# Second attention and last expert stage: two blocks in a row, or one block in which they take turns

## The reference, cut to what matters

```
x = x + xattn1(layernorm(x), ctx)          # 16 heads of 64, 64 context keys plus one null key, then a layernorm
n = x * rsqrt(mean(x^2) + 1e-8) * norm_w   # of layernorm(x)
x = x + relu(n @ sw1 + sb1) @ sw2 + sb2    # shared expert, all rows
      + sum over the 2 best of 8 experts of gate * (relu(n @ ew1[e] + eb1[e]) @ ew2[e] + eb2[e])
```

## Time and profile before

| | us |
|---|---|
| time, median of 3 runs | 1447.45 (1446.88 to 1448.34) |
| span of the profiled execution | 1468.5 |
| PE busy | 1250.4 (85%) |
| DVE busy | 1054.3 (72%) |
| ACT busy | 899.3 (61%) |
| POOL busy | 653.5 (44%) |

### The profile page before, as it was taken

The page is one execution under the profiler, slowest core; times in us unless marked ns, Lnnn a source line. Parts: engine busy times, 40 slices in busy tenths (PEclk is TensorE's granted clock), DMA queues, the critical chain, the costliest instruction groups (busy, mean ns, idle before and its releaser), DMA issues. The chain is left out here.

```text
span 1468.5 us, 35946 instructions
## 1 busy us (share of the span) xinstructions
PE 1250.4 (85%) x13401; PEld 1041.2 (71%) x13401; DVE 1054.3 (72%) x2080; ACT 899.3 (61%) x1699; POOL 653.5 (44%) x677
## 2 busy tenths in 40 slices
PE   4999998399999999997599999999997268999880
PEld 3777777278777877786489888888886256787660
DVE  5888888566877687675256678989887369676563
ACT  3888887566565666654355655666654248787660
POOL 2222222145655555564332345556755327165561
PEclk9999999689999999999699999999999669999995
DMA  4222221332213221321210000000000123146646
GB/s 143 93 94 93 94 93 64 116 94 80 73 39 92 80 73 37 94 80 44 86 38 17 10 17 9 17 15 18 24 13 17 44 58 89 48 151 217 203 139 182
DMA packets 88373, 109.64 MB, mean 75 GB/s; under 512 B 13322, under 2 KB 55050, under 8 KB 88202
## 3 DMA queue, kind: packets, MB, share of 16 engines
q1 hardware_dynamic: 83210, 97.05, 21.3%
q0 software_dynamic: 4992, 10.30, 2.1%
HBM read 61.70 MB, written 29.82 MB: 62 GB/s over the span
## 5 line engine op out<-in xcount | busy, mean ns | idle before, releaser
L830 POOL TENSOR_TENSOR b_h_lo<-b_h,b_h_hi 128x512 fp32r<-128x512 f32 x168 | 216.3, 1292 | 179.7 <-ACT b_h_hi L854 179.2
L849 ACT ACTIVATE b_zg<-b_zg 128x512 f32<-128x512 f32 x168 | 97.6, 581 | 82.0 <-PE b_zg L894 81.8
L854 ACT ACTIVATE b_h_hi<-b_h 128x512 fp32r<-128x512 f32 x168 | 105.2, 626 | 65.7 <-DVE b_h L1059 65.6
L1059 DVE TENSOR_TENSOR b_h<-b_zg,b_uw 128x512 f32<-128x512 f32 x168 | 116.2, 692 | 32.1 <-ACT b_zg L849 26.8
L2173 POOL DMA_INDIRECT planes_dram<-d_y_out,d_back x92 | 94.5, 1028 | 93.6 <-DVE d_y_out L2484 68.8
L1052 DVE TENSOR_TENSOR b_uw<-b_zu,b_gw 128x512 f32<-128x512 f32 x128 | 88.2, 689 | 57.7 <-PE b_zu L894 50.9
L2453 DVE TENSOR_TENSOR d_h_lo<-d_h,d_h_hi 128x512 fp32r<-128x512 f32 x124 | 85.1, 689 | 44.6 <-ACT d_h_hi L2214 26.8
L312 POOL TENSOR_TENSOR a_qx<-a_qT,headmask 128x256 f32<-128x256 f32 x64 | 37.9, 612 | 150.3 <-ACT a_qT L347 150.3
L519 DVE TENSOR_REDUCE a_top<-a_score_ps 128x8 f32<-128x1024 f32 x64 | 78.1, 1220 | 18.6 <-PE a_score_ps L410 18.6
L1293 POOL TENSOR_TENSOR c_prob<-c_prob,c_recip 128x512 f32<-128x512 f32 x64 | 65.5, 1044 | 50.9 <-DVE c_recip L1709 50.9
L1716 DVE TENSOR_TENSOR c_oT_lo<-c_oy,c_oT_hi 128x512 fp32r<-128x512 f32 x64 | 43.7, 683 | 58.1 <-ACT c_oT_hi L1421 57.5
(11 more groups left out here) (393 smaller groups left out, 4172.3 us busy)
## 6 DMA issues: line engine op xcount, KB each, us to landing
rows_dram<-a_blank SPq DMA_DIRECT2D x32, 520.0 KB, 3.3
b_gw<-gates_dram SPq DMA_DIRECT2D x64, 256.0 KB, 3.9
d_up_slot<-d_up_tab SPq DMA_DIRECT2D x15, 512.0 KB
d_down_slot<-d_down_tab SPq DMA_DIRECT2D x15, 512.0 KB
d_xg<-rows_dram SPq DMA_DIRECT2D x23, 260.0 KB
b_gm<-gates_dram SPq DMA_DIRECT2D x32, 160.0 KB, 3.8
c_craw<-in_c_ctxT_dram SPq DMA_DIRECT2D x16, 256.0 KB, 3.1
d_pay<-planes_dram SPq DMA_DIRECT2D x12, 256.0 KB, 4.3
```

Of the source, the lines that this page charges most:

```text
L830: pool.tensor_tensor(h_lo[:, m % HS, :], h[:, m % HF, :], h_hi[:, m % HS, :].bitcast(F32), ALU.subtract).then_inc(lo_done.sem, 1)
L849: act.activation(zg_ps[:, n % ZG, :], zg_ps[:, n % ZG, :], ACT.Silu).then_inc(sg_done.sem, 1)
L854: act.activation(h_hi[:, m % HS, :], h[:, m % HF, :], ACT.Copy).then_inc(hi_done.sem, 1)
L1059: dve.tensor_tensor(h[:, n % HF, :], zg_ps[:, n % ZG, :], uw[:, n % 2, :], ALU.mult).then_inc(h_done.sem, 1)
```

## The change

Both stages become generators, one for each engine, and share one block, one PSUM tensor (`arena`) and a memory plan (`Room`: the tiles of the last stage lie where tiles of the attention have been used up). `in_turn` runs them in a written order. The attention runs 38 ticks alone, -6 to 31 (ACT 37). Then steps of the last stage and ticks take turns:

```diff
+        order = [(1, 4), (0, 1), (1, 4)] + [(0, 1), (1, 3)] * 5 + [(0, 1), (1, 1)] * 3
+        for quarters in (1, 2, 1, 2, 1, 2, 1, 2, 2):
+            order += [(0, 1), (1, quarters)]
+        order.append((1, 4 * (TILES + 3)))
+        alone = 38
...
+            in_turn([(0, alone - 1)] + order, first.scalar(act), second.scalar(act))
...
+            in_turn([(0, alone)] + order, first.vector(dve), second.vector(dve))
```

All eight groups are routed by the attention; the router of the last stage, its three `pay` buffers and its `scattered` waits go:

```diff
-ROUTED = 5
...
-        ticks = range(-6, UNITS + 8)
+    ticks = range(-6, UNITS + 18)
...
-            return g if odd == 0 and 0 <= g < ROUTED else None
+        return g if odd == 0 and 0 <= g < GROUPS else None
+
+    def wait_scattered(eng, g):
+
+        eng.wait_ge(scattered[g % 2], 16 * 2 * GROUP * (g // 2 + 1))
...
-                    if g is not None and g + 1 < ROUTED:
+                if g is not None:
                         scatter(g, lo, hi)
...
                 act.wait_ge(r_scaled.sem, r_scaled.at(g + 1))
                 if g:
-                    act.wait_ge(scattered, 16 * 2 * GROUP * g)
+                wait_scattered(act, g - 1)
...
             def place(g):
                 if g:
-                    dve.wait_ge(scattered, 16 * 2 * GROUP * g)
+                wait_scattered(dve, g - 1)
```

The scale and shift of each row (`rstd`, `shift`) now come from the routing and not from a pass of their own (`finish_stats` with `rms`), and the shared jobs take the groups in the order 0 to 7. The last stage waits for the attention where it takes over its memory:

```diff
+        sp.wait_ge(marks["q_made"].sem, marks["q_made"].at(2 * UNITS))
+        sp.wait_ge(marks["k_made"].sem, marks["k_made"].at(2 * UNITS))
+        weights.sync(sp, 0, EARLY)
...
+        for k, c in steps:
+            if (k, c) == (0, 0):
+                act.wait_ge(marks["valued"].sem, marks["valued"].at(2 * UNITS))
+                act.wait_ge(marks["projected"].sem, marks["projected"].at(UNITS // 2))
...
+            dve.wait_ge(marks["r_scaled"].sem, marks["r_scaled"].at(g + 1))
```

In every job, and not only from job 8 on, the ReLU of step c = 3 is DVE's:

```diff
-        def on_dve(k, c):
+    def on_dve(c):
 
-            return k >= FIRST and c == CH - 1
+        return c == CH - 1
```

The final fetches go to rows of the expert table, which is free by then, and all sixteen are issued first:

```diff
-            for g in range(PAY):
-                fetch(g)
             for g in range(GROUPS):
                 sp.wait_ge(summed.sem, summed.at(2 * g + 2))
-                if g + PAY < GROUPS:
-                    fetch(g + PAY)
                 sp.dma_start(out[g * COLS:(g + 1) * COLS, :].rearrange("(u p) f -> p u f", p=P),
```

More of the change, by code:

```diff
@@ L104, in stage, with __init__, sb, in_turn @@
         earlier.replace(taken, held)
+class Room:
+    def __init__(self, nc, at, size):
+        self.nc, self.at, self.end = nc, at, at + size
+    def sb(self, name, shape, dt=F32):
+        size = -(-4 * int(np.prod(shape[1:])) // 32) * 32
+        assert self.at + size <= self.end, name
+        tensor = self.nc.alloc_sbuf_tensor_at(name, shape, dt, offset=self.at)
+        self.at += size
+        return tensor
+Programs = namedtuple("Programs", "sync gpsimd scalar tensor vector")
+def in_turn(order, first, second):
+    stages = (first, second)
+    for which, steps in order:
+        for _ in range(steps):
+            next(stages[which], None)
 class Mark:
@@ new lines, in sorted_experts, with share @@
+    jobs = []
+    for e in range(E + 1):
+        for m, (shared, name) in enumerate(((up_shared, "d_w"), (down_shared, "d_wd"))):
+            row = tab[:, e - 1, m, :] if e else shared[:, :]
+            jobs += pieces(row[:, 0:half], row[:, half:W], a[name][:, e * half:(e + 1) * half])
+    weights = SplitWeights(nc, ctx, tag + "sw", jobs, 3, sw_raw)
+    EARLY = 2
+    def share(k, c):
+        if k == -START:
+            return (0, EARLY) if c == 0 else (0, 0)
+        n, steps = len(jobs) - EARLY, 7 * CH
+        s = min(k * CH + c, steps)
+        if s < 0:
+            return (0, 0)
+        return EARLY + n * s // steps, EARLY + n * min(s + 1, steps) // steps
@@ new lines, in parts, with block_of, bias @@
+    def parts(shared, m, slots, k):
+        if k < FIRST:
+            return shared[:, :]
+        return tab[:, k - FIRST, m, :] if k < MOVED else slots[:, (k - MOVED) % WS, :]
+    def block_of(row, lo, c):
+        return row[:, lo * half + c * P:lo * half + (c + 1) * P]
+    def bias(k, c):
+        if k < FIRST:
+            return b_shared[:, c:c + 1]
+        return b_tab[:, k - FIRST, c:c + 1] if k < MOVED else b_slot[:, (k - MOVED) % (WS + 1), c:c + 1]
+    def on_dve(c):
+        return c == CH - 1
@@ new lines, in gpsimd @@
+    def gpsimd(pool):
+        for k, c in steps:
+            weights.rest(pool, *share(k, c), True)
+            t = k - 2 - FIRST
+            if 0 <= t < TILES and c == 0:
+                pool.wait_ge(out_done.sem, out_done.at(FIRST + t + 1))
+                pool.wait_ge(tail_done.sem, tail_done.at(t + 1))
+                for u in range(GROUP):
+                    pool.indirect_dma_start(
+                        planes, bass.IndirectOffsetOnAxis(ap=back[:, t, u:u + 1], axis=0),
+                        y_out[:, t % 2, u, :], None).then_inc(added[t % 2], 16)
+            yield
@@ L2144, in _ @@
[L2144 to L2150 removed]
+            in_turn([(0, alone)] + order, first.sync(sp), second.sync(sp))
         @block.gpsimd
@@ L2177, in _ @@
-            for i in range(2 * GROUP):
-                u, n = divmod(i, 2)
-                pool.indirect_dma_start(rows, bass.IndirectOffsetOnAxis(ap=route.dest[:, n, u:u + 1], axis=0),
-                                        route.pay[:, n, u, :], None).then_inc(scattered_last, 16)
-            ticks(step)
+            in_turn([(0, alone)] + order, first.gpsimd(pool), second.gpsimd(pool))
         @block.scalar
         def _(act):
-            for m in (xhi_done, twin_done, sig_done, h_act, hi_done, y_done):
-                m.credit(act)
@@ L2508, in program @@
+    earlier.sems = [s for s in earlier.sems if s not in finished]
 def program(nc, a, rows, gates, planes, out):
```

2255 lines of the change are left out of this document (1049 added, 1206 removed).

## The result

The changed kernel takes 1482.24 us (1481.11 to 1483.03) against 1447.16 (1446.48 to 1448.34): ratio 1.0239 [1.0223, 1.0254], 35 us slower. The forecast said slower, but 1453 us and at most 1470.

The account below looks back on a forecast made before the run. The prediction took latency, not work, as the bound: serial routing of groups 5 to 7 through one `pay` buffer. +7.5 us there less 2 at the end gave +5.5, so 1453 us, range 1432 to 1470.

Parts of the forecast that it names:

- the thread: Routing of groups 5 to 7 with one `pay` buffer: ends at 1263 against 1255.5, +7.5 us.
- Part (a): From tick 32 to `add_up` of group 7: DVE's work plus waits and collisions put `add_up` at 1192.
- and 4 for the collisions: Before `add_up` of group 7: 4 us lost where POOL's multiplies and table pieces hold DVE.
- ports collide: Rival, chance 0.16: multiplies of groups 5 to 7 hold DVE 1.5 to 2.4 us each; switch at 1275, time 1465.
- Part (b): From `add_up` of group 7 to the first turn of `xg`: POOL's work, landings, fills and hand-overs take 71 us.
- fit in beside: Behind `add_up`: the 24 remaining job steps fit beside the routing, PE needing about 1.4 us for each.
- The end, 2 us: End of the kernel: issuing all fetches first gains 0 to 4 us, taken as 2.

Follow-up runs that it names:

- no_pool_tab: The changed kernel with POOL's six table pieces given to DVE; 1476.61 us, ratio 1.0206 to the kernel before.
- best1: Changed kernel with later job steps, second `pay` buffer, ReLUs and `xn` on ACT, two steps behind the last scatters, table pieces on DVE; 1451.15 us, ratio 1.0034.
- jobs_after: The changed kernel with all ticks first, then all jobs, in the one block, no taking of turns; 1478.90 us, ratio 1.0223.
- the partner near the median: The profile of end_alone, used in place of the first profile of the kernel before; span 1446.4 us, time 1448.24.
- half_router: The changed kernel with the router's multiply and reduce over 64 of the 128 columns; 1462.62 us, ratio 1.0110.
- dve_mult: The changed kernel with the router's multiply of groups 5 to 7 on DVE and not on POOL; 1473.89 us, ratio 1.0184.
- before_again: The unchanged kernel before, profiled a second time in a slower batch; 1457.60 us in one run, no ratio.
- before_end: The kernel before with all sixteen final fetches issued first, in a slower batch; 1462.96 us, ratio 0.9987.
- end_alone: The kernel before with all sixteen final fetches issued first, as in the changed kernel; 1446.52 us, ratio 1.0000.

## Why the prediction was right in direction and wrong in size

- **What bounds it, and the thread: right.** Sums were 109.7 us on DVE (forecast 107; its own items make 104.5, since the 2.3 us of statistics were not taken off), 74.6 on ACT (73), 82.3 on POOL (84); none is near 153. DVE's work without the 21.3 us of collisions is 88, so that its forecast was near for a wrong reason. PE idles 6.84 us before the turn, 81.8 us after `add_up`, and both `fill` wait for a DMA, as it said they would.
- **Part (a), `add_up` at 1192: the step that failed is "and 4 for the collisions".** From tick 31 it allowed 62.7 us; it was 71.1. DVE's busy time there is 57.4, of which 13.8 are collisions, so the work is 43.6 against 45.5 forecast, and idle and start 13.7 against 13.2 (62.7 less 49.5). The 8.4 us missing are 9.8 of collisions, less 1.9 of work, and 0.5. The price was sized on large operations of two inputs in SBUF, with six multiplies at half; these six cost 9.1 us of their 14.2, and places beside POOL's other work 4.7. But reduces kept their 1.2 us, and operations of 32 columns were held as long as a multiply lasts, and `xn`, with one tensor in, too: four took 3.14 us at 1146.15 and 1.11 elsewhere. The Trainium skill says in "SBUF — State Buffer", section "SBUF: two separate sides", that the loser of the shared port pair blocks fully; the rows of 0.19 us that took 2.39 agree. It also says that the one which starts first has the pair; by the starts in the profile that does not hold here, since DVE's piece at 1129.58 (3.08 us) and the one of the earlier trace rows began 0.46 and 0.28 us before POOL's work and were the ones held. The forecast had given the case of colliding ports ("ports collide", `add_up` at 1200 to 1206, turn at 1275, 1465) 0.16; it was the nearest, and still 17 us short (`add_up` came at 1198.9).
- **Part (b), 71 us: 81.8.** Scatters of group 5 landed at 36.8 us and not 31.4: 1.7 us of collision in `xn` at 1200.1 and 3.2 in `logits` (1.41 and 2.21 us at 1207.7 and 1209.2) stand ahead of them. Those of group 6 then began at 48.6 us and not 37.7, 5.5 more, since `compare` of group 7 stands ahead of them and waited 12.0 us for DVE. ACT's exponentials were done at 1240.5, but DVE's `probabilities` came at 1245.7, behind 4.7 us of job steps that began when ACT had made its part of a table piece, at 1241.0. The prediction named table pieces as 1.3 us of execution each; that one holds a queue until another engine is ready was not in it. no_pool_tab and best1 price it on POOL at 5 and 10 us, the 1.3 us of each piece included.
- **What steps cost the thread.** The prediction let the 24 remaining steps "fit in beside". jobs_after shows that they don't: without them the thread to the last scatter is 16 us shorter.
- **Base.** The shown profile had a turn 126.5 us after tick 31 and 184 us of jobs behind; in the partner near the median it is 123.3 and 170.7. The sum was made against the first, which against this partner hid 3.2 us (against the two other profiles nothing, 126.0 and 127.0); 2.7 more came in the jobs behind, and 2.2 before tick 31. This is in the direction of the 5 us that half_router gained there, but one profile each can't tell it from scatter.
- **The end, 2 us: 0.**

Together: 19.2 us in (a) and (b), 3.2 and 2.7 of base and jobs, 2.2 ahead, 2.0 at the end: 29.3, against 29.2 missing (1482.2 less 1453). All but (a), (b) and the end depend on the one partner; the 19.2 in the thread is the main part with any of them.

Undoing it gives the same list from the other side: later steps and a second buffer 16.7, DVE lighter 1.5 and the tail 2.7, table pieces 10, multiplies 4.8: 35.7, by medians across batches.

## What to carry to other kernels

When two stages share in-order engines, work that fills a hole on PE can make the thread behind it longer by as much, as here. Before merging, write down for each engine what stands ahead of every link of the slowest thread, and count waits on other engines, not only durations: a 1.3 us piece of background work stood up to 8.6 us at the head of POOL's queue, and taking six such pieces away gave 5 us in one kernel and 10 in another. Run the order without any interleaving as well; if it is as fast, the interleaving has hidden nothing on balance.

Where POOL works beside DVE, take the full length of each elementwise pass of POOL as what it can cost DVE at worst, whatever the size of the DVE operation; here ten multiplies cost 13.4 of their 23.6 us, and the worst place 2.4 us beside 2.06 of POOL's. Moving such a pass to DVE at half its length can win though DVE is the fullest engine (dve_mult, 8 us).

## What the runs showed of the hardware that was not expected

DVE operations with one tensor input were held beside POOL too: `xn` and `y_sb` (`y_sb`, four of 128x128: 2.13 us at 1187.87 and 1.50 at 1139.30 beside a multiply, 1.12 alone), but not reduces from SBUF (two took 2.34 us with a multiply beside the second, one alone 1.22) and not reads of PSUM (`d_h` 0.74 to 0.75 throughout, beside POOL's `compare` at 1178.8 and its table piece at 1255.3 too).

The stretch of jobs 8 to 30 of one and the same kernel took 184 us in one profile and 171 in another (before_again; 182.5 and 170.7 in before_end and end_alone, which are one kernel as well), with PE at 11.9 of 15 us where it is otherwise full. A profile well above the median of its runs should not be the base of a sum.
